# One float32 product in place of three rounded ones in the expert layer of a recurrent block

## What is computed

```python
x = L0_attn_x
xn = _layernorm(x, axis=-1)
x = x + _L0_attn_ref(xn, ...) + _L0_ffn_ref(xn, Wr, W1, W2)
```

```python
xe = xf[dispatch]
h = jnp.maximum(jnp.einsum('ecd,edf->ecf', xe, W1), 0.0)
ye = jnp.einsum('ecf,efd->ecd', h, W2)
ye = ye * (pe * valid.astype(ye.dtype))[:, :, None]
y = jnp.zeros((t, d)).at[dispatch.reshape(-1)].add(ye.reshape(E * cap, d))
```

## Time and profile before

| | us |
|---|---|
| median of 3 runs | 165.67 (165.46 to 167.71) |
| profiled execution, its own time | 165.59 |
| span of that execution, first to last instruction | 163.8 |
| TensorE, VectorE, ScalarE, GpSimd busy | 124.8, 93.5, 86.2, 83.2 |
| mean granted TensorE clock, share of 2.4 GHz | 0.878 |

### The profile page before, as it was taken

The page is one execution under the profiler, slowest core; times in us unless marked ns, Lnnn a source line. Parts: engine busy times, 40 slices in busy tenths (PEclk is TensorE's granted clock), DMA queues, the critical chain, the costliest instruction groups (busy, mean ns, idle before and its releaser), DMA issues.

```text
span 163.8 us, 2058 instructions
## 1 busy us (share of the span) xinstructions
PE 124.8 (76%) x684; PEld 98.2 (60%) x684; DVE 93.5 (57%) x207; ACT 86.2 (53%) x197; POOL 83.2 (51%) x102
## 2 busy tenths in 40 slices
PE   5966999999995991699999739896979967941000
PEld 5956999836533890439659318694968956930000
DVE  4179300399898000861512410768948999299990
ACT  3047625014554840648685363999608958635650
POOL 7069640000477774377477876377765807560000
PEclk9997555579999999569999999999999999999555
DMA  4898699970011211011011111011110100116997
GB/s 133 231 270 315 268 356 342 399 318 2 16 48 36 54 58 48 18 49 49 16 52 48 48 48 48 16 50 49 49 46 21 33 16 32 42 58 183 327 301 214
DMA packets 14346, 19.27 MB, mean 118 GB/s; under 512 B 1664, under 2 KB 10112, under 8 KB 14336
## 3 DMA queue, kind: packets, MB, share of 16 engines
q1 hardware_dynamic: 9888, 13.63, 24.5%
q0 software_dynamic: 2048, 4.20, 8.7%
q10 hardware_dynamic: 2400, 1.32, 3.0%
HBM read 10.76 MB, written 8.39 MB: 117 GB/s over the span
## 4 chain that ended last, share of the span: by engine, by line
PE 40%; DVE 24%; DMA 8%; issue 8%; ACT 7%; another core or an unknown queue 6%; POOL 3%; POOLq 1%; SPq 0%; DVEq 0%; ACTq 0%
PE bank L495 8%; PE bank L427 7%; PE bank L385 7%; DVE xnT L869 5%; DMA x_tok<-in_x 4%; PE bank L395 4%; DVE xc L838 4%; PE bank L482 3%; DVE inp L865 3%; PE bank L416 3%; PE bank L484 2%; PE bank L483 2%; DVE dec L922 2%; DMA dec<-y_rows 2%
## 5 line engine op out<-in xcount | busy, mean ns | idle before, releaser
L357 POOL DMA_INDIRECT y_rows<-xn_tok,idx_out x32 | 37.1, 1159 | 25.2 <-DVE xn_tok L876 15.9
L350 POOL DMA_INDIRECT xn_tok<-xn_rows,idx_in x32 | 32.1, 1002 | 29.9 <-DVE idx_out L801 20.4
L618 ACT ACTIVATE h_sb<-bank 128x512 f32<-128x512 f32 x32 | 18.1, 596 | 25.7 <-PE bank L484 16.8
L495 PE MATMUL bank<-w_raw,h_sb 128*128 128x128 f32 x256 | 30.2, 275 | 0.1
L495 PEld LDWEIGHTS bank<-w_raw,h_sb 128*128 128x128 f32 x256 | 29.2, 192 | 0.2 <-issue 0.2
L482 PE MATMUL bank<-xg_hi,w_hi 128*128 128x512 f32 x32 | 14.0, 437 | 12.0 <-ACT h_sb L618 5.4
L427 PE MATMUL bank<-xc,par 128*128 128x512 f32 x32 | 17.2, 670 | 3.0 <-issue 2.8
L845 DVE TENSOR_TENSOR xg_lo<-bank,xg_hi 128x512 fp32r<-128x512 f32 x8 | 5.5, 688 | 18.6 <-ACT xg_hi L612 14.2
L876 DVE COPY xn_tok<-bank 128x512 f32<-128x512 f32 x7 | 4.8, 684 | 18.2 <-remote 11.3
L482 PEld LDWEIGHTS bank<-xg_hi,w_hi 128*128 128x128 f32 x32 | 6.1, 191 | 14.9 <-ACT h_sb L618 6.8
L427 PEld LDWEIGHTS bank<-xc,par 128*128 128x128 f32 x32 | 6.6, 214 | 12.0 <-issue 11.0
(11 more groups left out here) (111 smaller groups left out, 211.8 us busy)
## 6 DMA issues: line engine op xcount, KB each, us to landing
w_raw<-in_weights SPq DMA_DIRECT2D x8, 512.0 KB, 7.5
y_rows<-sca SPq DMA_DIRECT2D x4, 512.0 KB, 5.8
dec<-y_rows SPq DMA_DIRECT2D x8, 256.0 KB, 5.0
x_tok<-in_x SPq DMA_DIRECT2D x3, 512.0 KB, 9.4
xn_rows<-xn_tok SPq DMA_DIRECT2D x3, 512.0 KB, 3.5
out<-dec SPq DMA_DIRECT2D x4, 256.0 KB, 3.0
out<-dec ACTq DMA_DIRECT2D x4, 256.0 KB, 3.2
x_tok<-in_x SPq DMA_DIRECT2D x2, 256.0 KB, 5.4
```

The source lines that it names most:

```text
L350: g.indirect_dma_start(gathered[:, s * D:(s + 1) * D], None, xn_rows, bass.IndirectOffsetOnAxis(ap=idx_in[:, s:s + 1], axis=0)).then_inc(g ...
L357: g.indirect_dma_start(y_rows, bass.IndirectOffsetOnAxis(ap=idx_out[:, s:s + 1], axis=0), gathered[:, s * D:(s + 1) * D], None).then_inc(s ...
L495: last = mm(tile_of(e, s), h_sb[:, k * CAP + s * P:k * CAP + (s + 1) * P], w_raw[:, e, F + k * D:F + (k + 1) * D], start=(k == 0), stop=(k ...
L618: a(h_sb[:, k * CAP:(k + 1) * CAP], hbank[n % 3][:, :], ACT.Relu).then_inc(h_done, 1)
```

## The change

The float32r tensors `w_hi`, `w_lo`, `xg_hi` and `xg_lo` go, with their semaphores, and so do the functions `lead`, `weights_rest` and `columns_rest` with all their calls (8 each). ScalarE copies the gathered columns in float32 to `xgT`, which has two buffers. A block of the upward product is one float32 matmul with the weights as loaded. `turn(e)` waits for `columns(e-1)` only.

```diff
-        w_hi = sb("w_hi", [P, 2, F], F32R)
-        w_lo = sb("w_lo", [P, 2, F], F32R)
-        xg_hi = sb("xg_hi", [P, CAP], F32R)
-        xg_lo = sb("xg_lo", [P, CAP], F32R)
+        xgT = sb("xgT", [P, 2, CAP])
...
-                    pe.wait_ge(xg_lo_done, e)
+                    pe.wait_ge(xg_done, e)
...
             def up(e):
-                pe.wait_ge(xg_lo_done, e + 1)
-                pe.wait_ge(w_lo_done, e + 1)
+                pe.wait_ge(xg_done, e + 1)
+                pe.wait_ge(w_in[e], 16)
                 for k in range(KF):
                     n = e * KF + k
                     if n >= 3:
                         pe.wait_ge(h_done, n - 2)
-                    b = hbank[n % 3][:, :]
-                    w = slice(k * P, (k + 1) * P)
-                    mm(b, w_hi[:, e % 2, w], xg_hi[:, :], start=True, stop=False)
-                    mm(b, w_hi[:, e % 2, w], xg_lo[:, :], start=False, stop=False)
-                    mm(b, w_lo[:, e % 2, w], xg_hi[:, :], start=False, stop=True).then_inc(h_mm, 1)
+                    mm(hbank[n % 3][:, :], w_raw[:, e, k * P:(k + 1) * P], xgT[:, e % 2, :],
+                       start=True, stop=True).then_inc(h_mm, 1)
...
-            def lead(e):
-                act.wait_ge(w_in[e], 16)
+            def columns(e):
+                act.wait_ge(xg_tp, e + 1)
                 if e >= 2:
                     act.wait_ge(h_mm, KF * (e - 1))
-                a(w_hi[:, e % 2, :], w_raw[:, e, 0:F], ACT.Copy).then_inc(w_hi_done, 1)
-
-            def columns(e):
-                act.wait_ge(xg_tp, e + 1)
-                a(xg_hi[:, :], xg_bank[:, :], ACT.Copy).then_inc(xg_done, 1)
+                a(xgT[:, e % 2, :], xg_bank[:, :], ACT.Copy).then_inc(xg_done, 1)
...
-            def weights_rest(e):
-                dve.wait_ge(w_hi_done, e + 1)
-                v.tensor_tensor(w_lo[:, e % 2, :], w_raw[:, e, 0:F], w_hi[:, e % 2, :].bitcast(F32),
-                                ALU.subtract).then_inc(w_lo_done, 1)
...
-            def columns_rest(e):
-                dve.wait_ge(xg_done, e + 1)
-                v.tensor_tensor(xg_lo[:, :], xg_bank[:, :], xg_hi[:, :].bitcast(F32),
-                                ALU.subtract).then_inc(xg_lo_done, 1)
```

More of the change, by code:

```diff
@@ L8 @@
 F16 = mybir.dt.float16
-F32R = mybir.dt.float32r
 ALU = mybir.AluOpType
@@ L211, in rglru_moe_kernel @@
         gather_in = [sem(f"gather_in{e}") for e in range(E)]
-        w_hi_done = sem("w_hi_done")
-        w_lo_done = sem("w_lo_done")
         xg_tp = sem("xg_tp")
         xg_done = sem("xg_done")
-        xg_lo_done = sem("xg_lo_done")
         h_mm = sem("h_mm")
@@ L637, in _ @@
             biased(0)
-            lead(0)
-            lead(1)
             act.wait_ge(coef, 5)
@@ L654, in _ @@
                     relu(e + 1)
-                if e + 2 < E:
-                    lead(e + 2)
                 stages(ACT_AFTER, e, names)
@@ L807, in _ @@
             v.reciprocal(lna[:, 3:4], lna[:, 2:3]).then_inc(coef, 1)
-            def weights_rest(e):
-                dve.wait_ge(w_hi_done, e + 1)
-                v.tensor_tensor(w_lo[:, e % 2, :], w_raw[:, e, 0:F], w_hi[:, e % 2, :].bitcast(F32),
-                                ALU.subtract).then_inc(w_lo_done, 1)
-            weights_rest(0)
             kept = put(v.tensor_scalar(keep[:, :], hi16[:, :], float(CAP), None, ALU.is_lt))
@@ L901, in _ @@
             convolve(3, 4)
-            weights_rest(1)
             taps_of_chunk(2)
-            columns_rest(0)
             for e in range(E):
-                if e + 1 < E:
-                    columns_rest(e + 1)
                 stages(DVE_AT, e, names)
@@ L910, in _ @@
                 stages(DVE_LATE, e, names)
-                if e + 2 < E:
-                    weights_rest(e + 2)
                 stages(DVE_AFTER, e, names)
```

## The result

| | before | after |
|---|---|---|
| median of 20 runs, us | 166.03 (164.13 to 167.71) | 165.91 (165.12 to 166.52) |
| ratio of undisturbed runs | | 1.0138 (95%: 1.0095 to 1.0181) |
| profiled execution, its span, us | 165.59, 163.8 | 165.67, 163.8 |
| TensorE, VectorE, ScalarE busy, us | 124.8, 93.5, 86.2 | 129.2, 83.3, 82.4 |
| mean granted clock | 0.878 | 0.878 |

A forecast was written before the change was run, and what follows sets the result against it. It took TensorE as mostly busy in the loop, with waits for other engines, and VectorE as setting the end. About +0.5 us up to evict(5) and -1.2 on VectorE gave 165.6 - 0.7 = 164.9 us, range 159.5 to 169.0.

The forecast's parts named there:

- up(0): Expert 0's upward product: starts up to 0.9 us earlier, runs 0.7 us longer, the rest unusable; net 0.
- up(1): Expert 1's upward product: three blocks hidden by 4.88 us of idleness, only the fourth, at the lower clock, shows; +0.4 us.
- up(2): Expert 2's upward product: +0.7 us, less 0.32 of waiting for the relu and 0.2 from ScalarE's removed lead; together +0.2.
- up(3): Expert 3's upward product: three blocks covered by a 0.88 us wait, fourth +0.17, ScalarE's gates(3) 0.5 earlier; together -0.35 us.
- up(4) and up(5): Upward products of experts 4 and 5: +0.7 covered by a 0.86 us wait for xg_lo, then +0.17; together about +0.2 us.
- What one block costs: One upward block on TensorE: 0.86 us instead of 0.69, +0.17 for each of 32, 5.4 us in all; +0.43 at lower clock.
- VectorE from evict(5) on: VectorE's unbroken list near the end, for which project5 waits: two rest operations go, -1.2 us.
- Rival 1: All of TensorE's longer products come through: +5.4 us, 171.0 us; chance 0.14.
- Rival 2: Late completions, as behind down(0) and ahead of evict(5), shrink: 160.5 us, faster; chance 0.26.
- Rival 3: The last scatters wait for TensorE, not VectorE's rows2, so the -1.2 us falls away: 166.8 us; chance 0.10.

The follow-up runs named there:

- before_b: The kernel before, unchanged, run again for its trace on a chip without late completions: 150.66 us, ratio 1.001.
- after_b: The changed kernel, unchanged, on a chip without late completions: four runs, 151.40 to 155.30 us, against 150.44 for the kernel before; profiled 152.03.
- product_only: The kernel before with only the upward product made one float32 matmul per block, all copies, rests and waits kept: 153.39 us against 150.35, ratio 1.0208.
- wide_down_c: The changed kernel with down of experts 0 to 6 as four 512-column matmuls instead of 16 of 128, late chip: 159.12 us against 166.73 for the kernel before.
- scalar_kept_c: The changed kernel with ScalarE's eight lead copies put back, unread, on a late chip: 166.64 us, ratio 0.9833 against the kernel before.

## Why the prediction was wrong

I forecast 0.7 us less. The profiled pair shows 0.1 us more and the ratio 1.4% more. How far each step moved, in us; the sums are differences of the starts of the next `turn` or `down` in the timelines (the result's chip by the earlier trace rows and the profile after, the prompt one by `before_b` and `after_b`):

| step of the prediction | forecast | the result's chip | prompt chip |
|---|---|---|---|
| up(0) | 0 | -0.01 | +0.43 |
| up(1) | +0.4 | +0.54 | +0.54 |
| up(2) | +0.2 | +0.36 | +0.54 |
| up(3) | -0.35 | -2.03 | +0.56 |
| up(4) and up(5) | +0.2 | +1.20 | +0.32 |
| from there to `evict(5)` | 0 | +1.15 | -0.87 |
| VectorE from `evict(5)` to `project5`, or to down(7) | -1.2 | -1.21 | +0.01 |
| sum | -0.7 | 0.0 | +1.5 |

The lines on which the reading of `up(3)` rests: `gates(3)` on TensorE before, ScalarE's relu ahead of it before, and `gates(3)` on TensorE after.

```profile
97.14 1.96 PE L427 MATMUL bank<-xc,par 128*128 128x512 f32 x4 [2.77 <-issue]
```
```profile
95.31 0.60 ACT L618 ACTIVATE h_sb<-bank 128x512 f32<-128x512 f32 x1 [0.82 <-remote]
```
```profile
94.11 3.85 PE L420 MATMUL bank<-xc,par 128*128 128x512 f32 x8
```

- **What one block costs** was right: two records 0.43 us apart. At the lower clock the block of `up(1)` took 1.86 us to the start of the gates (67.02 to 68.88), where I had 1.72, and the old one 1.44 (66.80 to 68.24), where I had 1.29: +0.42, as forecast. By the Trainium skill ("FP8 and Floating Point Precision", "TensorE Precision Notes") true float32 takes four passes, which with the 216 ns of its page "TensorE: Matmul & The Clock Gate" ("Back-to-back issue gap") give an estimate of 0.86 us for the new block, and this agrees; the sum over all blocks of 6.9 us that followed with 216 ns for the old ones doesn't, for `before_b` and `product_only` differ by 0.69 us an expert, 5.5 us over eight.
- ***up(1)*, *up(2)*.** Near: 0.54 instead of 0.4, and 0.36 instead of 0.2. The cover was as described.
- ***up(3)*.** Wrong. On the result's chip the kernel before had 2.77 us of idleness inside `gates(3)`, which my sum left out. It came from ScalarE's relu of the last block of `up(3)`, which began 2.6 us behind that block's records. After, `gates(3)` has no gap. In return `down(3)` of after was seen 3.5 us late where it had been 0.7, and -2.03 is followed by +1.20. That these two nearly cancel, so that the records stand at +0.06 at `turn(6)` where I had about +0.5, is luck. On the prompt chip the step was +0.56: the wait ahead of the fourth block that I counted as cover (0.88 us) was itself a late completion, and isn't there.
- ***VectorE from evict(5) on*.** On the result's chip the -1.2 is exact: 1.21. The step that failed stands just ahead of it: "Up to here the step from `up(1)` sums to 0.4 + 0.2 - 0.35 + 0.2 = about +0.5." I let that step carry over into `evict(5)`, which waits for `down(5)`'s completion. Its records stood still (+0.06 at `turn(6)`), but the completion was 4.9 us late instead of 3.6, so `evict(5)` moved by +1.21 and took the whole -1.2 (0.8 us of it go with GpSimd's later stop, shown above). On the prompt chip the -1.2 failed itself: `down(7)` there waits for TensorE's products, and the step was +0.01. I had listed "new ones of several us arise behind other `down` steps" as what would break the forecast; they came behind `down(2)` and `down(3)` (2.8 and 3.5 us), and this one by 1.2 us.
- **Rival 1** is what a prompt chip shows in the middle of the loop, TensorE busy without a gap through `up(1)` to `up(3)`, at under a third of its price: 1.5 of 5.5 us. By the same starts 0.3 us is absorbed at `up(0)`, 0.4 in `up(1)` to `up(3)`, 1.1 in `up(4)` and `up(5)`, 0.9 in `up(6)` and `up(7)`, and 1.3 between them and `down(7)`; among it are waits of the kernel before for VectorE's rests (0.87 us ahead of `up(5)`) and rows (0.85 ahead of `project5`).
- **Rival 2** fell: the late completions behind the `down` steps grew, from about 13 us in all to 19.
- **Rival 3** has the right mechanism on the prompt chip: the end waits for TensorE, `project3` to `project5` run as one (L499 x24), and VectorE's saving isn't on the path. On the result's chip `project5` still waits for VectorE.

The 1.4% itself isn't split by these runs: the profiled pair, equal to 0.1 us, doesn't show it, and another set on a late chip gave 1.0017. That the product costs about 2% where completions are prompt is shown (`product_only`); that this is the 1.4% of the result is an argument only.

## What to carry to other kernels

Cost a swap of instructions on the busiest engine against a profile in which the waits are its own. A wait that has no visible releaser is poor cover: here such waits came, went and moved by microseconds under every edit, so a product that leans on one is better costed in full. When a bound engine gets the longer instructions and another the shorter list, ask which of the two ends the chain at each place after the change; here the 10 us taken off VectorE and 4 off ScalarE gave back about 1.5 us on a prompt chip, where the product cost 3.3.

## What the runs showed of the hardware

- The same kernel takes 150.4 us on two chips and 162 to 167 on at least two others, with nearly the same mean granted clock (0.871 in `before_b`, 0.878 before), and on one of the late ones 165.87 us in one set and 161.91 in another. The difference is in completions of TensorE's work that other engines see up to 6.5 us after the records end; on the prompt chips none that an engine waited for was over 0.3 us late.
- On the late chips `evict`, where its wait ended in a remote release, started 1.2 to 2.4 us after the end of GpSimd's last indirect DMA issue in a row, in all traces but two places (2.6 us in `wide_down_c`, and amid a row in `scalar_kept_c`). That is where the releases fall, not a shown cause.
- A hole of 4.6 to 4.9 us on TensorE was followed by the clock's lower level (granted 0.50, 1.2 GHz) from about 65.8 to 72.5 us, and the gates behind it took 5.59 us for eight records against 3.85.
